# Matching edges to nodes on VectorE: eight operations of 80 columns with a scalar per partition in place of one of 640 columns

## The reference

```python
deg = jnp.maximum(segment_sum(ones, dst), 1.0);  deg_isqrt = deg ** -0.5
h = relu(layernorm(x));  x = x + segment_sum(edge_weight[:, None] * h[src], dst) @ W0.T + b0
h = relu(layernorm(x))
for i in range(5):
    W = (ssp(rbf @ fw1[i] + fb1[i]) @ fw2[i] + fb2[i]) * C[:, None]     # rbf, C: functions of edge_weight
    agg = segment_sum((h @ lin1[i])[src] * W, dst) / deg
    h = layernorm(h + ssp(agg) @ lin2[i] + lin2_b[i]) * ln_g[i] + ln_b[i]
x = x + h
h = relu(layernorm(x))
e = tanh(s_dst[dst] + s_src[src] + gate_b) * deg_isqrt[dst] * deg_isqrt[src] * edge_weight
x = x + segment_sum(h[src] * e[:, None], dst)
h = relu(layernorm(x));  x = x + segment_sum(h[src], dst) @ W3.T + b3
```

## Time and profile before

| | us |
|---|---|
| median of 3 runs (4480.47 to 4484.24) | 4482.3 |
| profiled execution | 4474.97 |
| its span, first to last instruction | 4473.2 |
| busy in it: GpSimd | 3286.1 |
| TensorE | 2497.9 |
| ScalarE | 2152.7 |
| VectorE | 1966.4 |

### The profile page before, as it was taken

One profiled execution on the slowest core, in us unless ns is written; L12 is line 12 of the kernel. 1 busy time (PEld: TensorE's weight loads), 2 busy tenths in 40 slices (PEclk: granted clock), 3 DMA queues, 4 the chain that ended last, 5 costly groups with the idle time before them and its releaser, 6 DMA issues. The chain is left out here.

```text
span 4473.2 us, 53257 instructions
## 1 busy us (share of the span) xinstructions
PE 2497.9 (56%) x13164; PEld 2226.0 (50%) x13164; DVE 1966.4 (44%) x4507; ACT 2152.7 (48%) x5584; POOL 3286.1 (73%) x3339
## 2 busy tenths in 40 slices
PE   2554456666566665666656666566773333334433
PEld 2544456655465554555545555455662333333333
DVE  3222155555555555555555555566663222211111
ACT  3444456665556655566555665556653545510000
POOL 5777767777677776777767777677775777767776
PEclk8555567777677776777767777676665555555555
DMA  6333222222222222222222222222221222212222
GB/s 131 105 92 97 77 63 68 70 68 57 63 67 69 68 57 64 66 69 68 57 63 67 68 70 57 60 69 67 68 57 39 58 57 58 56 48 56 56 56 54
DMA packets 193622, 297.24 MB, mean 66 GB/s; under 512 B 81669, under 2 KB 116194, under 8 KB 193302
## 3 DMA queue, kind: packets, MB, share of 16 engines
q0 software_dynamic: 106496, 219.17, 19.1%
q10 hardware_dynamic: 33974, 57.75, 4.6%
q1 hardware_dynamic: 52832, 16.73, 1.6%
HBM read 272.15 MB, written 21.27 MB: 66 GB/s over the span
## 5 line engine op out<-in xcount | busy, mean ns | idle before, releaser
L598 POOL DMA_INDIRECT rows<-table,staged_src x3328 | 3279.4, 985 | 1171.3 <-issue 890.5
L770 PE MATMUL pD<-scatter,msg 128*128 128x80 f32 x4160 | 756.9, 358 | 718.5 <-PEq L768 709.4
L770 PEld LDWEIGHTS pD<-scatter,msg 128*128 128x128 f32 x4160 | 714.4, 267 | 790.6 <-issue 790.6
L691 PE MATMUL pD<-scatter,rows 128*128 128x80 f32 x2496 | 572.7, 424 | 686.6 <-PEq L683 375.7
L762 PE MATMUL pC<-fw,hidden 128*128 (+1 forms) x4160 | 810.4, 370 | 182.4 <-PEq L760 180.8
L691 PEld LDWEIGHTS pD<-scatter,rows 128*128 128x128 f32 x2496 | 545.2, 331 | 712.0 <-issue 712.0
L762 PEld LDWEIGHTS pC<-fw,hidden 128*128 128x128 f32 x4160 | 755.4, 278 | 218.4 <-issue 217.5
L908 ACT ACTIVATE scatter<-onehot,c_e 128x80 f32<-128x80 bf16 x2080 | 549.4, 346 | 581.4 <-ACTq L906 581.4
L1346 DVE TENSOR_TENSOR msg<-msg,rows 128x512 f32<-128x512 f32 x520 | 337.0, 689 | 719.2 <-DVEq L1140 711.9
L1136 DVE COPY staged_src<-src_i 128x8 int32<-128x8 int32 x416 | 73.7, 177 | 827.3 <-DVEq L1148 827.3
L942 ACT ACTIVATE hidden<-hidden 128x512 f32<-128x512 f32 x520 | 327.5, 630 | 63.6 <-ACTq L833 3.6
(11 more groups left out here) (195 smaller groups left out, 1732.1 us busy)
## 6 DMA issues: line engine op xcount, KB each, us to landing
rows<-table,staged_src POOLq DMA_INDIRECT x3328, 2.5
basis<-basis_d ACTq DMA_DIRECT2D x130, 256.0 KB, 2.8
table<-node_rows SPq DMA_DIRECT2D x66, 128.0 KB, 1.8
msg<-in_edge_weight_dram ACTq DMA_DIRECT2D x54, 128.0 KB, 3.4
basis_d<-basis ACTq DMA_DIRECT2D x26, 256.0 KB, 3.6
hidden<-in_edge_weight_dram ACTq DMA_DIRECT2D x48, 128.0 KB, 3.1
table<-node_rows SPq DMA_DIRECT2D x11, 132.0 KB, 2.4
out_dram<-node_rows SPq DMA_DIRECT2D x11, 128.0 KB, 1.8
```

Source lines behind the costliest of these rows:

```text
L598: pool.indirect_dma_start(out=rows[:, s, j, 0:width], out_offset=None, in_=tab[:, :], in_offset=bass.IndirectOffsetOnAxis(ap=staged_src[:, ...
L691: mm = pe.matmul(sum_ps, rows[:, g % RING, j, 0:D], scatter[:, g % 2, j, :], start=(j == 0), stop=(j == CH - 1))
L770: mm = pe.matmul(sum_ps, msg_of(g, h)[:, c * D:(c + 1) * D], scatter[:, g % 2, HALF * h + c, :], start=(h == 0 and c == 0), stop=(h == 1 a ...
```

## The change

`match` becomes a loop over the eight chunks. Each operation compares the 80 window numbers with one column of `dst_rel`, given as a scalar of each partition, and writes the 80 columns of its chunk. The last of them is returned, so what follows a match (its semaphore, a wait for it) hangs on the last one. The comparison, the outputs and the place of the match in VectorE's order stay.

```diff
                 def match(dst, g):
-                    return dve.tensor_tensor(dst, over_chunks(win[:, :]), per_chunk(dst_rel, g), ALU.is_equal)
+                    for j in range(CH):
+                        ins = dve.tensor_scalar(dst[:, j, :], win[:, :], dst_rel[:, g * CH + j:g * CH + j + 1], None, ALU.is_equal)
+                    return ins
```

## The result

The changed kernel took **4444.66 us** (median of 4 runs, 4443.87 to 4446.13); the kernel before, run beside it, took 4481.81 (4480.47 to 4484.24). The ratio is 0.9917, with a 95% interval of 0.9905 to 0.993: faster by 0.7 to 0.95%. The forecast was 4451.

A forecast was written before the change was run, and what follows sets the result against it. GpSimd's 3328 gathers set the pace. From the 4482.3 us median, -39.1 (match's hold) + 5.0 (new operations) + 2.5 (boundaries) = -31.6 gave 4451 us; the range for 8 in 10 was 4439 to 4482.

The forecast's parts named there:

- -39.1 us for the match's hold: Inside passes: the old two-input match lengthens 143 gathers by over 20 ns, 39.1 us in all, which the change removes.
- +5.0 for the new operations: Gathers beside the new match: short double-rate operations hold the port 42 ns of every 175, costing 5.0 us over 416 groups.
- 2.4 requests a group: Gathers ask twice, early and for a later stretch, so a 1.48 us train of eight operations meets 2.4 requests.
- +2.5 for the boundaries: Between passes: the longer match delays VectorE's chain before the next pass's first gather, 2.5 us together, from 0 to 5.
- The four that I priced at 0.4 each: Four boundaries at layer ends: of the match's extra 0.66 us, 0.28 is absorbed, leaving +0.4 us at each.
- The 0.28 us that I counted as absorbed: Wait ahead of L1154 at a layer's end, taken to absorb 0.28 of the match's extra 0.66 us.
- ±0 for moved operations: Two-input operations behind the match come 0.66 us later and meet gathers elsewhere: 0, within 3.7 us either way.
- The port held through the train: Each new match operation keeps the port until the next has it: +48 us, 4530; chance 12%.
- Single rate: New match operations run at single rate, 295 ns each, and hold no port: -35 us, 4447; chance 15%.
- No change by late VectorE: Gain lost again: holds near 90 ns with later boundaries, or late VectorE's two-input operations meet more gathers: 4482; chance 11%.

The follow-up runs named there:

- r2: Changed kernel's loop of eight 80-column operations, but each with two SBUF tensor inputs (destination column broadcast) instead of a scalar per partition: 4487.29 us, ratio 1.0013 to the kernel before.
- r3: Changed kernel with the match as one 640-column operation with one scalar per partition, seven of eight comparisons left out: 4450.41 us, ratio 0.9935 to the kernel before.
- r4: Changed kernel with every match made twice, the first time into a spare tile: 4466.23 us, ratio 0.9967 to the kernel before.
- r11: Changed kernel with every match made twice, the first time into a spare tile, run again without an edit: 4456.19 us, run once.
- r1: The change undone, that is the kernel before once more: 4481.63 us, ratio 1.0001.
- r8: Changed kernel with the old 640-column match for the last two groups of each pass alone: 4436.71 us, ratio 0.9913 to the kernel before.
- r5: Changed kernel's 80-column loop with two SBUF inputs per operation, VectorE waiting for each before the next: 4496.64 us, ratio 1.0046 to the kernel before.
- r9: Changed kernel, 3200-column boundary operations cut by tile, waits behind tiles of two-input rows there, old match for each pass's last two groups: 4414.84 us, ratio 0.985.
- r10: The kernel before, run a third time without an edit to see its median undisturbed gather: 4473.53 us.
- r12: Changed kernel with one 640-column, one-scalar match (seven of eight comparisons left out), run again without an edit: 4439.51 us, run once.

## Why the prediction was right, step by step

**-39.1 us for the match's hold: right.** Measured in the profile: 39.1 to 1.2 us by the match, 35.0 over all gathers. r2 shows that splitting does not free them while the second SBUF input stays, r3 that dropping it brings nearly all of the gain even in one piece. The reading of the earlier trace rows was correct.

**+5.0 for the new operations: the mis-sized term.** It was 1.2 us in 31 gathers. The prediction had 2.4 requests a group meet holds of 42 ns, 5.0 ns each on average. Of the late requests none shows a lengthening over 20 ns, though 348 trains ran across one; there it is VectorE that waits (671 operations of over 0.3 us, the mean operation 285 ns beside a median of 253). In r3 a double-rate operation of 545 ns does hold late requests (59 of them), so a late request can be held; that the length of a single operation decides is the likely reason. The doubled match (r4 and r11: 1.0 us) puts this term near zero.

**+2.5 for the boundaries: too small, 4.5 (inside its range of 0 to 5).** The four that I priced at 0.4 each rose by 0.46 to 0.68, the second layer's last pass by 1.4 instead of 1.0, and the first layer's end, which I held to have idle time ahead, by 1.6, of which r1 shows 1.0 without the change (16.92 instead of 15.94). r8 takes 3.3 of it back. The 0.28 us that I counted as absorbed stand in front of L1156 as they stood in front of L1154 ("issue"), so nothing was absorbed there. The pause alone also misleads at these four. From the end of a pass's last gather to the end of the next pass's first it is 16.51 + 3.55 = 20.06 us before and 17.00 + 4.01 = 21.01 after, 0.95 more. Against that, the last eight gathers of the pass are together some 0.45 us shorter, and VectorE's chain, which starts at the rows of the group before them, comes no sooner for it (in the first of the four its messages start 8.82 us ahead of the last gather's end before, 8.35 after). What is left is 0.5 at each, close to the 0.4.

**±0 for moved operations: about right**, +2.9 net in the gathers outside the match: the messages +0.8, the first 3200-column row of four boundaries +1.7 (the longer first gathers just named), `softplus` of the nodes -1.2, and +1.6 in small ones. r4, r5 and r9 show that this term is the one that grows when VectorE has more to do.

**The sum** was -31.6; the profiles differ by -30.5, the medians by -37.2. That the sum fits the profiles to 1.1 us is partly luck: its small terms were off by -3.8, +2.0 and +2.9 and nearly cancel. The profiled execution of before lay 7 us below its median, that of after at its median (4444.43 of 4444.66), and I had carried the same distance over to the forecast. In the runs beside r1 the kernel before spreads over 10 us (4475.97 to 4485.96, 21 runs), the changed one over 2.3 (4 runs). r10 to r12 show one thing that differs so without an edit, the undisturbed gather, with 5 to 7 us over 3328 of them; the holds of the match differ by 4.5 us between two profiles of the kernel before. How much of either was in the timed runs no profile shows, so the 6.7 us between the profiles' difference and the medians' stay open. The chip is a rival that no run excludes: the kernel before had medians of 4475.8 on one chip and of 4481.33 and 4483.52 on another, and on which chip its first profile was taken is not on record.

**The rivals.** The port held through the train: fell, for this form. It does happen, in r2, for the form with two inputs. In the Trainium skill, "SBUF — State Buffer", section "Who interferes with whom", whoever issues first in a two-port mode has the shared ports for the whole instruction. r3 agrees (33 and 196 ns over, to the match's end), and the prediction rightly stopped the rule at the instruction, not the train. The same section of the Trainium skill has an instruction with two SBUF inputs contend with a GpSimd instruction that reads SBUF, not with one that only writes it, and infers that two-tensor operations leave descriptor generation alone. The inference does not hold for these gathers (329 held in r2 for 46.8 us), which read their indices from `staged_src`. The rule in front of it fits the early request alone being held (143 gathers in r1, and none of 290 at the late one); that the one is a read and the other a write, no run shows. Single rate: fell, the 253 ns are those of double rate. No change by late VectorE: not here (the messages lengthen 240 gathers, it was 241), but this is what r5 and r9 ran into.

## What to carry to other kernels

Where GpSimd's gathers set the pace, cost VectorE's work by what it holds, not by its busy time: eight operations of 1.45 us together with one tensor input beat one of 0.81 us with two. Splitting helps only in a form that lets the other engine in between operations, so look at whether a held gather ends with the operation or with the row. Before giving an engine more to do because it is idle, find the stages where it is not (here the last pass of the second layer and the groups ahead of a boundary), and keep the old form there.

## What was not expected of the hardware

- Operations with two SBUF inputs that follow each other without a wait can hold a gather through several of them: to the end of a train in 286 of 329 cases (up to 0.66 us within one train of eight, 1.19 us where a second train followed at once), and 2.8 us in a row of 25. With a wait between (0.15 us) it goes on at the end of the running one, in 131 of 131.
- Operations with one SBUF tensor and scalars per partition that overlap just as much let it in: 0.94 to 1.06 us beside four rows of 25.
- The same undisturbed gather has a median of 944 ns in one execution and 946 or 947 in another of the same kernel, which over 3328 of them is 5 to 7 us. What sets it is open.
- A gather's two requests are held by different operations: the early one, within 0.1 us of its start, by both forms; the late one, 0.8 us in, only by the double-rate form (59 gathers of r3, none of r1 and r2). Short double-rate operations do not hold the late one (none of 348 trains): they wait for it themselves, 671 of 3328 of them.
